# Moving row 0's third product, row 1's second turn, the next pair's first turn and two ACT steps inside the MLP pairs of a four-layer graph network

## What is computed

```python
h = jax.nn.relu(_ln(h @ w1 + b1, g1, be1))
h = jax.nn.relu(_ln(h @ w2 + b2, g2, be2))
y = h @ w3 + b3
out = x + y
out = _ln(out, bn_g, bn_b)
return jax.nn.relu(out)
```

## Time and profile before

| | |
|---|---|
| median of 3 runs | 4356.87 us (4340.77 to 4359.95) |
| the profiled execution, its own time | 4392.47 us |
| its span, first to last instruction | 4390.6 us |
| PE busy | 3205.5 us, 73% |
| DVE busy | 2064.2 us, 47% |
| ACT busy | 1234.4 us, 28% |
| POOL busy | 996.7 us, 23% |
| mean granted TensorE clock over the span | 0.837 |

### The profile page before, as it was taken

The page is one execution under the profiler, slowest core; times in us unless marked ns, Lnnn a source line. Parts: engine busy times, 40 slices in busy tenths (PEclk is TensorE's granted clock), DMA queues, the critical chain, the costliest instruction groups (busy, mean ns, idle before and its releaser), DMA issues.

```text
span 4390.6 us, 50246 instructions
## 1 busy us (share of the span) xinstructions
PE 3205.5 (73%) x15864; PEld 1988.1 (45%) x15864; DVE 2064.2 (47%) x5603; ACT 1234.4 (28%) x3451; POOL 996.7 (23%) x1015
## 2 busy tenths in 40 slices
PE   3888277777771101052999997899899999957999
PEld 3444144444440000021899982444555555534445
DVE  6778366676661000043575551543344444464334
ACT  1222255555550010021344430300133333343000
POOL 0000655555557777634000000000000000000000
PEclk6999688888885555565899998899999999978999
DMA  4434333344330000000111127333200000001232
GB/s 96 136 136 147 107 114 116 119 121 127 117 114 6 0 0 1 0 1 4 25 35 34 35 79 276 94 101 103 92 6 6 5 5 5 5 28 48 87 103 87
DMA packets 232495, 298.66 MB, mean 68 GB/s; under 512 B 109094, under 2 KB 156891, under 8 KB 228187
## 3 DMA queue, kind: packets, MB, share of 16 engines
q1 hardware_dynamic: 187995, 197.27, 14.9%
q0 software_dynamic: 39968, 66.75, 5.8%
q10 hardware_dynamic: 4320, 31.95, 1.8%
HBM read 222.45 MB, written 73.40 MB: 67 GB/s over the span
## 4 chain that ended last, share of the span: by engine, by line
PE 45%; DVE 20%; another core or an unknown queue 16%; issue 8%; ACT 4%; DVEq 3%; DMA 3%; POOL 1%; SPq 0%; ACTq 0%
PE PS L1006 11%; PE PS L874 9%; PE PS L860 5%; PE PS L847 5%; PE PS L699 5%; PE PS L817 4%; DVE SUMS L1236 3%; DVE SUMS L1448 2%; DMA BG<-a_d 2%; DVEq L1381 2%; PE PS L815 2%; DVE SUMS L1367 2%; DVE SUMS L1365 2%; DVE OHB L1243 1%
## 5 line engine op out<-in xcount | busy, mean ns | idle before, releaser
L1365 DVE TENSOR_TENSOR SUMS<-SUMS,PS 128x384 f32 x500 | 276.5, 553 | 764.7 <-remote 612.4
L457 POOL DMA_INDIRECT BG<-feat_d,IDXST x500 | 484.8, 970 | 378.4 <-PE PS L699 238.4
L1006 PE MATMUL PS<-BG,SL 128*128 128x512 f32 (+1 forms) x1440 | 534.3, 528 | 26.6 <-ACT SL L640 26.6
L485 POOL DMA_INDIRECT a_d<-VAL,IDXS x499 | 500.4, 1003 | 221.4 <-issue 158.2
L815 PE MATMUL PS<-OHB,SL 128*5 128x128 f32 x1000 | 220.1, 307 | 401.2 <-DVE SUMS L1367 182.9
L561 ACT ACTIVATE BG<-BG,SL 128x64 f32<-128x64 f32 x2000 | 489.6, 335 | 70.2 <-issue 70.2
L817 PE MATMUL PS<-OHB,BG 128*128 128x128 f32 x2000 | 425.7, 342 | 45.9 <-issue 45.9
L699 PE MATMUL PS<-IDENT,SUMS 128*128 128x128 f32 (+3 forms) x736 | 202.5, 310 | 348.3 <-issue 102.1
L492 POOL MEMSET SUMS<- 128x7760 f32 x1 | 6.6, 6565 | 1861.2 <-PE PS L1006 1861.2
L817 PEld LDWEIGHTS PS<-OHB,BG 128*128 128x128 f32 x2000 | 315.6, 225 | 179.4 <-issue 179.4
L1006 PEld LDWEIGHTS PS<-BG,SL 128*128 128x128 f32 x1440 | 272.2, 192 | 262.6 <-issue 212.7
(11 more groups left out here) (266 smaller groups left out, 4329.4 us busy)
## 6 DMA issues: line engine op xcount, KB each, us to landing
BG<-a_d SPq DMA_DIRECT2D x171, 256.0 KB, 4.2
a_d<-SUMS SPq DMA_DIRECT2D x30, 1088.0 KB
feat_d<-SUMS ACTq DMA_DIRECT2D x30, 1040.0 KB, 4.6
AL<-a_d SPq DMA_DIRECT2D x104, 256.0 KB, 2.6
SL<-a_d SPq DMA_DIRECT2D x85, 256.0 KB, 2.6
BG<-rel_d SPq DMA_DIRECT2D x100, 160.0 KB, 3.1
BG<-in_edge_attr_dram SPq DMA_DIRECT2D x124, 128.0 KB, 2.2
BG<-feat_d,IDXST POOLq DMA_INDIRECT x500
```

What stands on the lines that cost most here:

```text
L457: pool.indirect_dma_start(RING[:, t // NB % 3, t % NB, :], None, table, bass.IndirectOffsetOnAxis(ap=IDXST[:, t:t + 1], axis=0),).then_inc ...
L485: pool.indirect_dma_start(a_d.rearrange("n (w o) -> (n w) o", o=1), bass.IndirectOffsetOnAxis(ap=IDXS[:, t:t + 1], axis=0), VAL[:, t:t + 1 ...
L1006: last = pe.matmul(PS[:, to + q, 0:width], lhs[:, i, c, :], w[:, c, q * width:(q + 1) * width], start=(c == 0), stop=(c == kc - 1))
L1365: add = tt(a, a, PS[:, AGG_BANKS[n % 4], 0:3 * P].rearrange("p (a n) -> p a n", a=3), ALU.add)
```

## The change

On PE, row 0's third product `dense3(0, j)` moves up: it stood behind row 1's second turn `turn_hidden(1, j, 1)` and `edge_part(1, j + 1)`, and stands now ahead of both. The next pair's first turn, `turn_hidden(0, j + 1, 0)`, leaves the top of the pair and stands ahead of row 1's third product `dense3(1, j)`; the first one goes ahead of the loop. On ACT, `hidden_relu(0, j + 1, 0)` leaves the top of the pair and stands between the two output roots. No instruction is added or removed.

```diff
@@ ACT
+            def out_root(i, j):
+                act.wait_ge(s(f"y_var{i}"), j + 1)
+                act.activation(YM[:, i, 2:3], YM[:, i, 1:2], ACT.Sqrt, bias=EPSC[:, 0:1]).then_inc(s(f"y_sqrt{i}"), 1)
...
             def dense_pair(j, more):
-                hidden_relu(0, j, 0)
                 hidden_norm(1, j, 0)
...
                 hidden_relu(1, j, 1)
                 if more:
                     hidden_norm(0, j + 1, 0)
-                for i in range(2):
-                    act.wait_ge(s(f"y_var{i}"), j + 1)
-                    act.activation(YM[:, i, 2:3], YM[:, i, 1:2], ACT.Sqrt, bias=EPSC[:, 0:1]).then_inc(s(f"y_sqrt{i}"), 1)
+                out_root(0, j)
+                if more:
+                    hidden_relu(0, j + 1, 0)
+                out_root(1, j)
 
             hidden_norm(0, 0, 0)
+            hidden_relu(0, 0, 0)
@@ PE
             def dense_pair(j, more):
 
-                turn_hidden(0, j, 0)
                 dense1(1, j)
                 dense2(0, j, 0)
                 turn_hidden(1, j, 0)
...
                 dense2(1, j, 1)
                 if more:
                     dense1(0, j + 1)
+                dense3(0, j)
                 turn_hidden(1, j, 1)
                 if more:
                     edge_part(1, j + 1)
-                dense3(0, j)
+                    turn_hidden(0, j + 1, 0)
                 dense3(1, j)
 
             edge_part(0, 0)
             edge_part(1, 0)
             dense1(0, 0)
+            turn_hidden(0, 0, 0)
             pe.wait_ge(s("mlp_late"), 16 * KH)
```

## The result

| | before | changed |
|---|---|---|
| median | 4357.35 us (4340.77 to 4360.78, 6 runs) | 4381.85 us (4373.14 to 4389.29, 6 runs) |
| ratio | | 1.0066, 95% interval 1.0045 to 1.0086 |
| the profiled execution, its own time | 4392.47 us | 4381.02 us |
| its span | 4390.6 us | 4379.1 us |

The changed kernel is 24.5 us slower by the medians, 0.66%. I had given 13.3 us, 0.3%, with a range to 4391: the time is inside the range and the direction is right.

What follows compares the result with a forecast made beforehand. PE was taken to bound the MLP pairs. Waits +1.8, clock +14.3 and last pair -2.8 summed to +13.3 us on a median of 4356.9: 4370.2 us, 0.3% slower, range 4354 to 4391.

Steps and rivals of the forecast that it cites:

- The old stalls go: PE's waits of 1.72 us ahead of row 1's second turn and 1.91 us ahead of row 0's dense2 vanish.
- One wait of 4.19 us comes: PE stands still 4.19 us ahead of the next pair's first turn, waiting for ACT's scaling of row 0.
- The chain's end: Row 1's turn at 3590.36, its relu, then row 0's scaling on ACT release PE's next first turn at 3596.31.
- +0.13 us a pair: Without the clock, a pair's lost time on PE goes from 4.12 to 4.25 us; +1.8 us over 14 pairs.
- Row 1's next turn has no wait: DVE's later row 1 output and stats would just be done when PE reaches row 1's next turn; costed at nothing.
- rival 4: DVE is late for row 1's next turn too: 0.6 us more a pair, 8.4 us on top, 4379; chance 6%.
- The cover: Slack on PE before row 1's next turn needs DVE's stats: used up to the tenth, both at 3611.0.
- The clock, +14.3 us: All 14 new PE stalls bring a clock fall at 1.5 us each: 21.0 less 6.7 paid now.
- the two rows for a long stall: The stage's two PE stalls over 5 us, both followed by 1.2 GHz: 1.35 us at 3895.01, 2.9 at 3137.47.
- Rival 3: Each clock fall behind PE's new stall costs as much as at 3137, 2.9 us: +33 us, 4390; chance 12%.
- the row at 3137.47: A PE stall of over 5 us ahead of row 0's first turn, whose clock fall cost 2.9 us.
- The last pair, -2.8 us: Its 5.15 us PE stall is filled by dense3, its clock fall likely goes; row 1's product reaches DVE 2.8 us earlier.

Runs made afterwards that it cites:

- the exchange of two steps: Changed kernel with ACT's scaling of the next pair's row 0 put ahead of row 1's relu: 4368.8 us, ratio 0.9944 to the kernel before.
- filled kernel: Changed kernel with four useless 128 x 512 products on PE between the edge part and the next first turn: 4347.01 us, ratio 0.9982 to the kernel before.
- the ACT part alone: Kernel before with only the relu of the next pair's row 0 moved between ACT's output roots: 4325.06 us, ratio 0.9924; measured again 4367.79 us, 0.9945.
- the PE part alone: Kernel before with only row 0's third product and the next first turn moved on PE, ACT as before: 4408.26 us, ratio 1.0123.

## Why the prediction was right, and where its size was off

*The old stalls go.* Right: no wait ahead of row 1's second turn and none ahead of dense2 of row 0.

*One wait of 4.19 us comes.* Right: 4.01 us in the profile, "about 4.0" as the profile counts it, 14 times, ended by ACT's scaling. The chain's end, 5.95 us behind row 1's turn (3596.31 - 3590.36), was 5.94 (3249.57 to 3255.51). That it is ACT's queue is shown by the exchange of two steps. Without the clock I had +0.13 us a pair, 1.8 us in all. The filled kernel has +0.11, and its 14 pairs together (710.73 us) are 1.8 us above those of the kernel before without their falls (715.61 - 6.7).

*Row 1's next turn has no wait.* Right: no wait. That isn't the slow PE's doing, which I had given as the reason against rival 4: in the filled kernel, at a clock of 1.00, PE doesn't wait there either. The cover is about nothing, as forecast; in the ACT part alone, where PE comes earlier, the wait is there with 0.76 us.

*The clock, +14.3 us.* This is the term that was off in size. That every one of the 14 stalls is followed by a fall was right. The price was not: I took 1.5 us, near the cheaper of the two rows for a long stall and the 1.68 of a short one, with the reason that part of the slow time lies inside a stall. Behind 3149.50 PE was busy for 5.8 us at a clock of 0.50, all of it work: the turn and the third product took 1.76 + 5.46 us instead of 0.93 + 3.455, 2.8 us more; behind 3203.12 it was 1.76 + 4.26, 1.6 us more. The mean over the 14 is 2.2, so the term is 14 x 2.2 - 6.7 = 24 us instead of 14.3; by the filled kernel it is 30.2 - 6.7 = 23.5. Rival 3, that each fall costs 2.9, was right for every second one.

The two long rows that I had were two samples of a wide spread. The first stall of the stage, always 5.15 to 5.24 us long and always ahead of the same turn, is in every trace here, and the dense1 behind it takes from 3.93 to 5.55 us (a price of 1.3 to 2.9 us): 5.55 in the kernel before, 4.40 in the changed one. So the row at 3137.47 was no better guide for standing at the same instruction. What was missing is that a single row prices no fall: the middle of the two, 2.1, would have given 23 us. Why the price varies, and why it alternates in the changed kernel, stays open. The rule from the Trainium skill ("TensorE: Matmul & The Clock Gate", "Why this matters for your kernels": no long idle gaps between bursts) told the number of falls, not their price. The trace agrees with it for the long stalls, 14 falls behind 14 of 4.01 us; the falls behind 1.91 and 2.09 us and behind 1.36 and 0.70 us are shorter idle times than it warns of.

*The last pair, -2.8 us.* Wrong, it was -0.2: from the pair's dense2 to the last write 52.3 us before (3860.38 to 3912.66) and 52.1 after (3847.50 to 3899.62). The timelines of PE and DVE there:

```profile
3882.04 1.09 PE L704 MATMUL PS<-IDENT,AL 128*128 128x128 f32 x8 [1.70 <-ACT AL L633]
3886.12 5.21 PE L1011 MATMUL PS<-BG,SL 128*128 128x256 f32 x16 [2.99 <-ACT SL L644]
```

```profile
3891.42 0.42 DVE L1590 TENSOR_TENSOR BG<-PS,BG 128x256 f32<-128x256 f32 x1 [2.52 <-PE PS L1011]
...
3893.95 4.30 DVE L1597 TENSOR_SCALAR BG<-BG,YM 128x256 f32<-128x256 f32 x1
```

The working had row 1's third product 4.09 us behind the turn, and it came 4.08 behind. What failed is "its fall of the clock likely goes": the product waits 2.99 us for its relu, the clock falls behind that wait, and the product reaches DVE 5.3 us behind its start (3886.12 to 3891.42) instead of 3.8. That took 1.5 us of the 2.8. Another 1.3 went on DVE, where L1597 takes 4.30 us instead of 3.04 beside POOL's memset (see below).

*The start.* From the first dense1 to the first dense2 it was 16.14 us before (3128.63 to 3144.77) and 14.91 after: -1.2 us. It is the spread of the price behind the first stall (dense1 5.55 and 4.40 us), not a part of the change.

Sum as measured: 14 pairs +25.3, of which 23.5 are the clock and 1.8 the wait; last pair -0.2; start -1.2: +24 us by the trace, 24.5 by the medians. The clock was 9.2 us too cheap and the last pair 2.6 us too good, both the same way, and the start, which I had at nothing, took 1.2 back. The time lies inside the range because its upper end had a price of 2.9 us for every fall.

## What to carry to other kernels

When a step is moved up into a gap, ask what the step was covering where it stood. Here one block of 3.45 us could cover either of two latencies; either of the two moves on PE, with the ACT part, was no slower than the kernel before, and both together left the longer latency bare. And price a stall on TensorE together with what follows it: two stalls of under 2 us cost this kernel less than one of 4 us with nearly the same sum, and filling that one with useless products was worth 30 us. If a trace has two rows for the same event with a factor of two between them, put both into the sum: here even the same stall at the same instruction had either price.

## What the runs showed of the hardware

How often the clock fell behind a wait of PE, over 14 pairs each: of 1.72 us never (the kernel before, the ACT part alone), of 1.91 us in 4, of 2.09 us in 10, of 4.01 us in all 14. The length of one wait doesn't settle it alone: with ACT's two steps exchanged it fell in 2 of 14 pairs behind 1.36 and 0.70 us, one turn apart. A fall cost 1.6 to 1.7 us behind the waits of 1.91 and 2.09 us, and 1.6 or 2.7 to 2.8 behind that of 4.01 us. In the PE part alone the same 4.01 us cost 1.7 in nine pairs, where the turn still ran at full speed (0.93 us) and only the product behind it was slow (5.15 us), and 2.4 or 2.7 in the other five. I had not expected the long stall to alternate between two prices.

DVE's L1597, a `tensor_scalar` on SBUF that takes 0.41 us elsewhere, took 4.30 us in the last pair and 3.04 in the kernel before (L1591 there). In both it ended 0.14 or 0.15 us behind POOL's memset, and in the other twelve traces 0.13 to 0.16 us behind it, though it had begun anywhere from 2.4 to 3.7 us into the memset. The memset runs from 3891.54 for 6.56 us here and from 3904.57 for 6.57 us there:

```profile
3891.54 6.56 POOL L492 MEMSET SUMS<- 128x7760 f32 x1 [1886.58 <-PE PS L1011]
```

The `tensor_tensor` and stats instructions of DVE beside the same memset kept their usual times (0.42 us for L1590 at 3891.42 and L1591 at 3891.88). So this one DVE instruction ended only with the memset, and starting it earlier gained nothing. Why it is that one wasn't tried; a kernel with the memset moved away was not run either.
